# A delta-rule scan on one core: the predictions as 16 products of 128 rows from a block-diagonal state, and solved matrices written row index innermost

## What is computed

```python
rk = x.reshape(Bb, Tt, H, dd)                    # of the layer-normed x
rk = rk / jnp.maximum(jnp.linalg.norm(rk, axis=-1, keepdims=True), 1e-12)
wk = jnp.pad(rk[:, :-1], ((0, 0), (1, 0), (0, 0), (0, 0)))
v = (x @ Wv.T).reshape(Bb, Tt, H, dd)
gate = jax.nn.sigmoid(x @ Wg.T)
beta = jax.nn.sigmoid(x @ Wb.T)
def step(S, inp):
    rk_t, wk_t, v_t, g_t, b_t = inp
    pred = jnp.einsum('bhk,bhkd->bhd', wk_t, S)
    err = (v_t - pred) * b_t[..., None]
    S = S + wk_t[..., None] * err[..., None, :]
    o = jnp.einsum('bhk,bhkd->bhd', rk_t, S) * g_t[..., None]
    return (S, o)
```

## Time and profile before

| | |
|---|---|
| median of 3 runs | 2370.92 us (2365.35 to 2374.8) |
| profiled execution, time | 2373.69 us |
| profiled execution, span | 2372.0 us |
| mean granted TensorE clock | 0.966 of full |
| PE busy | 2108.6 us, 61992 products |
| DVE busy | 1985.7 us |
| ACT, POOL busy | 1727.6 us, 1726.7 us |
| DMA engines, main queue | 30.0% of their time |
| issue of one `kbd` transfer to its landing | 2.0 us (median) |

### The profile page before, as it was taken

The page is one execution under the profiler, slowest core; times in us unless marked ns, Lnnn a source line. Parts: engine busy times, 40 slices in busy tenths (PEclk is TensorE's granted clock), DMA queues, the critical chain, the costliest instruction groups (busy, mean ns, idle before and its releaser), DMA issues. The chain is left out here.

```text
span 2372.0 us, 145909 instructions
## 1 busy us (share of the span) xinstructions
PE 2108.6 (89%) x61992; PEld 1334.4 (56%) x61992; DVE 1985.7 (84%) x5810; ACT 1727.6 (73%) x3628; POOL 1726.7 (73%) x3098
## 2 busy tenths in 40 slices
PE   1679999999999999999999999999999988499997
PEld 1355666566666665656666656666666655255554
DVE  5487899888898888988898888989988985488886
ACT  3767777777777777777777777877777743477775
POOL 2667888888888888888888888888888853144343
PEclk7789999999999999999999999999999997799999
DMA  2111222222222222222222222222222211478885
GB/s 86 51 43 58 76 79 77 75 75 76 78 77 75 74 76 75 76 75 76 76 78 77 75 75 77 78 75 77 77 80 77 59 61 49 151 196 231 227 229 131
DMA packets 132139, 215.53 MB, mean 91 GB/s; under 512 B 31353, under 2 KB 31361, under 8 KB 131489
## 3 DMA queue, kind: packets, MB, share of 16 engines
q1 hardware_dynamic: 131488, 206.20, 30.0%
HBM read 104.40 MB, written 67.11 MB: 72 GB/s over the span
## 5 line engine op out<-in xcount | busy, mean ns | idle before, releaser
L775 DVE TENSOR_TENSOR ps_elim<-ps_elim,sys 128x30 f32<-128x30 f32 (+14 forms) x1920 | 543.6, 326 | 0.8
L783 DVE TENSOR_TENSOR sys<-sys,ps_elim 128x30 f32<-128x30 f32 (+14 forms) x1920 | 534.8, 316 | 1.0
L900 PE MATMUL ps_v<-wv,xt 128*128 128x512 f16 x1536 | 429.7, 390 | 26.1 <-DMA kbd<-kt 13.5
L900 PE MATMUL ps_y<-wo,ot 128*128 128x512 f16 x1536 | 406.9, 388 | 11.6 <-DVE x L827 9.5
L927 PEld LDWEIGHTS ps_chain<-rhs,t_t 32*32 32x32 f32 x16384 | 263.4, 144 | 132.9 <-issue 131.6
L927 PE MATMUL ps_chain<-rhs,t_t 32*32 32x32 f32 x16384 | 296.1, 218 | 24.3 <-issue 18.4
L684 ACT ACTIVATE state<-ps_s 128x512 f32<-128x512 f32 x128 | 76.5, 598 | 265.0 <-PE ps_s L991 265.0
L921 PEld LDWEIGHTS ps_chain<-state,key_t 32*32 32x32 f32 x16384 | 174.8, 105 | 152.6 <-issue 151.1
L991 PEld LDWEIGHTS ps_s<-err,key_b 32*32 32x32 f32 x16384 | 172.6, 107 | 142.9 <-issue 142.3
L1277 PE MATMUL ps_f<-wq,f_xq 128*128 128x512 f16 x1024 | 242.6, 381 | 6.7 <-DVE f_xq L1243 6.7
L803 DVE TENSOR_TENSOR rhs<-val,ps_chain 128x512 f32<-128x512 f32 x128 | 88.0, 687 | 188.3 <-PE ps_chain L921 187.7
(11 more groups left out here) (159 smaller groups left out, 5072.2 us busy)
## 6 DMA issues: line engine op xcount, KB each, us to landing
x_in<-in_L_attn_x SPq DMA_DIRECT2D x128, 256.0 KB
kbd<-kt SPq DMA_DIRECT2D x512, 64.0 KB, 2.0
x_res<-in_L_attn_x SPq DMA_DIRECT2D x128, 256.0 KB
x_scratch<-x SPq DMA_DIRECT2D x128, 256.0 KB, 6.4
f_x<-x_scratch SPq DMA_DIRECT2D x32, 1024.0 KB, 7.7
out<-f_res SPq DMA_DIRECT2D x128, 256.0 KB, 3.8
gate<-gates SPq DMA_DIRECT2D x128, 7.9 KB
gate<-gates SPq DMA_DIRECT2D x128, 0.2 KB
```

Of the source, the lines that this page charges most:

```text
L775: dve.tensor_tensor(tmp, factors(r, c, first, end)[:, c - first:C - 1 - first, c - first:c - first + 1].to_broadcast(shape), sys[:, r, c:c ...
L783: dve.tensor_tensor(dst, dst, tmp, ALU.add).then_inc(elim_done[r], 1)
L900: last = pe.matmul(out, lhs[:, a, kb, :], weights[:, w, kb, :], start=(i == 0), stop=(i == 3 * KB - 1))
```

## The change

Four things change in `attention`.

First, the prediction. `key_t` and its transpose on DVE are gone. `predict` is now 16 products: for each group of 4 heads and each batch, `kt` (128 partitions, 32 columns) is stationary, and the moving side is `state_bd`, the state with its 32x32 blocks on a diagonal of 128 rows and 128 columns. `state_bd` is zeroed once by POOL; after every tile 16 transfers on SP, one for each batch and each head of a group, copy blocks of 32 partitions x 128 numbers from `state` into it. `update` writes its blocks in another order of columns, so that each transfer moves one run of 128 numbers. `kt` has 8 buffers instead of 2, `state` one instead of 2.

Second, the order. On PE, `predict` stands in one piece behind six value products, its waits ahead of the sixth; the second half of `update` comes after one output product instead of three, and the moved ones follow later. On SP, the gate move that waited for its forerunner is issued a step later, the load and the store of rows stand ahead of the `kbd` transfers, and the state's transfers come last in the step, behind `kbd`.

Third, the solved matrices. `t_t` is laid out with the row index innermost, so the 32 numbers that PE loads are neighbours, and DVE's transpose writes them 32 apart.

Fourth, small things: `x_res` has 4 buffers instead of 2, a dump buffer is shared, some semaphores are merged, and `feed_forward` zeroes `y_var` once.

The core of the diff:

```diff
-        t_t = sb("t_t", [P, 2, C, 2, H])
+        t_t = sb("t_t", [P, 2, 2, H, C])
-        state = sb("state", [P, 2, D])
+        state = sb("state", [P, D])
+        state_bd = sb("state_bd", [P, B, HB, KB * HD])
...
+                n, l, live = on(base, j, 0)
+                if live and n < NT - 1:
+                    wait(sp, s["state_done"], n + 1)
+                    for b in range(B):
+                        for i in range(HB):
+                            w = KB * HD * i
+                            sp.dma_start(state_bd[HD * i:HD * i + HD, b, i, :],
+                                         state[C * b:C * b + C, w:w + KB * HD]).then_inc(state_loaded[b][l % 2], 16)
...
-                    nc.scalar.activation(state[:, (l + 1) % 2, :], ps_s[:, :], ACT.Copy).then_inc(s["state_done"], 1)
+                    nc.scalar.activation(state[:, :], ps_s[:, :], ACT.Copy).then_inc(s["state_done"], 1)
...
-                    dve.transpose(t_t[:, r, :, :, :].rearrange("p i a h -> p i (a h)"), sys[:, r, :, :]).then_inc(s["tt_done"], 1)
+                    dve.transpose(t_t[:, r, :, :, :].rearrange("p a h i -> p i (a h)"), sys[:, r, :, :]).then_inc(s["tt_done"], 1)
...
-                    dve.transpose(key_t[:, l, :, :], heads(key[:, l % 2, :])).then_inc(s["keyt_done"], 1)
...
-                    wait(pe, s["state_done"], n + 1)
-                    wait(pe, s["keyt_done"], n + 1)
+                    wait(pe, s["kt_done"], n + 1)
...
+                        for b in range(B):
+                            pe.wait_ge(state_loaded[b][(n - 1) % 2], 64 * ((n - 1) // 2 + 1))
...
-                        for h, q, e in blocks(half):
-                            last = pe.matmul(ps_chain[q, e], key_t[q, l, h, :], state[q, l % 2, e], start=True, stop=True)
+                        for g in range(KB):
+                            for b in range(B):
+                                q, w = slice(C * b, C * b + C), slice(P * g, P * g + P)
+                                moving = state_bd[:, b, :, HD * g:HD * g + HD]
+                                last = pe.matmul(ps_chain[q, w], kt[:, l, g, q], moving, start=True, stop=True)
...
-                            last = pe.matmul(ps_chain[q, e], t_t[q, l // 2 % 2, :, l % 2, h], rhs[q, e], start=True, stop=True)
+                            last = pe.matmul(ps_chain[q, e], t_t[q, l // 2 % 2, l % 2, h, :], rhs[q, e], start=True, stop=True)
...
+                            col = HD * (h % HB * KB + h // HB)
+                            last = pe.matmul(ps_s[q, col:col + HD], key_b[q, l, e], err[q, l % 2, e],
```

More of the change, by code:

```diff
@@ L427, in step @@
                     sp.dma_start(tile(x_in, l % 4), rows(io["x"], base, j, LAG_LOAD)).then_inc(x_loaded[l % 4], 16)
+                n, l, live = on(base, j, LAG_GRAM - 1)
+                if live:
+                    wait(sp, s["gate_moved"], n * 16 + 16)
+                    if isinstance(n, int) and n == 0:
+                        sp.wait_ge(s["zeros"], 3)
+                    sp.dma_start(gate[0:P:C, l, :], gates[C - 1:P:C, (l - 1) % 8, H:2 * H]).then_inc(gate_done[l], 16)
                 n, l, live = on(base, j, LAG_GRAM)
@@ L431, in step @@
                     sp.dma_start(gate[1:P, l, :], gates[0:P - 1, l, H:2 * H]).then_inc(s["gate_moved"], 16)
[L432 to L442, removed]
-                                     kt[HD * i:HD * i + HD, l % 2, :, :]).then_inc(kbd_loaded[l % 2], 16)
                 n, l, live = on(base, j, LAG_Y)
                 if live:
-                    wait(sp, s["x1_done"], n - 1)
-                    sp.dma_start(tile(x_res, l % 2), rows(io["x"], base, j, LAG_Y)).then_inc(res_loaded[l % 2], 16)
+                    wait(sp, s["x1_done"], n - 3)
+                    sp.dma_start(tile(x_res, l % 4), rows(io["x"], base, j, LAG_Y)).then_inc(res_loaded[l % 4], 16)
                 n, l, live = on(base, j, LAG_STATS2)
@@ L452, in step @@
                                  x1[:, l % 4, :]).then_inc(x1_stored[l % 4], 16)
+                n, l, live = on(base, j, LAG_V)
+                if live:
+                    if isinstance(n, int) and n == 0:
+                        sp.wait_ge(s["zeros"], 3)
+                    wait(sp, s["kt_done"], n + 1)
+                    for i in range(HB):
+                        sp.dma_start(kbd[HD * i:HD * i + HD, l % 2, i, :, :],
+                                     kt[HD * i:HD * i + HD, l, :, :]).then_inc(kbd_loaded[l % 2], 16)
+                n, l, live = on(base, j, 0)
+                if live and n < NT - 1:
+                    wait(sp, s["state_done"], n + 1)
+                    for b in range(B):
+                        for i in range(HB):
+                            w = KB * HD * i
+                            sp.dma_start(state_bd[HD * i:HD * i + HD, b, i, :],
+                                         state[C * b:C * b + C, w:w + KB * HD]).then_inc(state_loaded[b][l % 2], 16)
             run(step)
@@ L458, in _ @@
         def _(pool):
-            pool.memset(state[:, 0, :], 0.0).then_inc(s["state_done"], 1)
-            pool.memset(kbd[:, :, :, :, :], 0.0).then_inc(s["kbd_zero"], 1)
-            pool.memset(gates[:, BODY - 1, :], 0.0).then_inc(s["first_gate"], 1)
+            pool.memset(state_bd[:, :, :, :], 0.0).then_inc(s["zeros"], 1)
+            pool.memset(kbd[:, :, :, :, :], 0.0).then_inc(s["zeros"], 1)
+            pool.memset(gates[:, BODY - 1, :], 0.0).then_inc(s["zeros"], 1)
             def step(base, j):
@@ L935, in step @@
                     wait(pe, s["xt_done"], upto(v + 2))
-                value(0, SHARE)
-                last = predict(1)
+                value(0, 2 * SHARE - 1)
+                chain_ready(base, j)
+                value(2 * SHARE - 1, 2 * SHARE)
+                last = predict()
                 if live:
                     last.then_inc(s["pred_psum"], 1)
-                value(SHARE, 2 * SHARE - 1)
                 gram_ready(base, j)
-                value(2 * SHARE - 1, 2 * SHARE)
                 if m_live:
@@ L947, in step @@
                             out = ps_gram[q, :].rearrange("p (i h) -> p h i", h=H)[:, HB * g:HB * g + HB, :]
-                            last = pe.matmul(out, kt[:, m_l % 2, g, q], kbd[:, m_l % 2, :, g, q], start=True, stop=True)
+                            last = pe.matmul(out, kt[:, m_l, g, q], kbd[:, m_l % 2, :, g, q], start=True, stop=True)
                     last.then_inc(s["gram_psum"], 1)
```

74 lines of the change are left out of this document (34 added, 40 removed).

## The result

| | before | changed |
|---|---|---|
| median | 2369.65 us (4 runs) | 3562.83 us (4 runs, 3560.83 to 3564.15) |
| ratio, 95% interval | | 1.5033 [1.5001, 1.5065] |
| profiled execution | 2373.69 us | 3564.15 us |
| mean granted clock | 0.966 | 0.802 |

The change makes the kernel 50% slower. The forecast was 3895 us within 3350 to 4300: the direction and the mechanism were as predicted, the time forecast was 9% too long.

What follows compares the result with a forecast made beforehand. PE's work in written order was taken to bound the kernel at 14.78 us a step; the new transfer link would make the loop 26.7 us. 507.3 + 127 x 26.7, less 2.8, gave 3895 us, range 3350 to 4300.

Steps and rivals of the forecast that it cites:

- held up behind `kbd`: On SP, the state's first transfer waits for the four `kbd` issues ahead of it: 0.6 to 1.5 us, taken as 0.7.
- The link: From state's copy to prediction: 16 transfers issued in series on SP, then landing; takes 15 us and nothing hides it.
- the spacing: On SP, time from one state transfer's issue to the next: 0.62 to 0.92 us, taken as 0.77, 11.55 for 15.
- The clock: PE's clock falls in its pauses, so its 8.6 us in the loop cost 2.4 us more (bounds 0 and 8.6).
- the drain: Drain of the pipeline in the profiled kernel: 65 us with PE busy 49.06 and granted clock 0.77 of full.
- Gaps: PE's issue gaps in the loop: taken as 0.8 us a step, bounds 0 and 1.
- PE's saving: PE's step loses 0.4 us (prediction), 0.7 (solve's layout) and a tenth for issue gaps: 1.2 us, leaving 13.6.
- PE's work in its order sets the pace: Kernel before, steady stretch: PE's work in written order bounds the 14.78 us step, and the scan's loop just fits.
- Hidden transfers: Rival 1: transfers are hidden and PE stays the bound, 2219 us, needing 0.08 us an issue; chance 4%.
- rival (3): Clock stays at 2.4 GHz or SP issues at the faster spacing: 22.4 to 25 us, 3350 to 3680 us; chance 20%.
- the forecast's own: Case (4), the forecast itself: 25 to 28.5 us a step, 3680 to 4125 us; chance 60%.
- all of PE's work in the loop at 1.2 GHz: Rival (6): PE's loop work runs wholly at the low clock, 32.9 us a step, 4680 us; chance 4%.

Runs made afterwards that it cites:

- half_count: Changed kernel with only 8 of the 16 state transfers in each step, that part of the computation left out: 2899.52 us, ratio 1.2181.
- half_bytes: Changed kernel with all 16 state transfers, each of 64 numbers a row instead of 128: 3559.96 us, ratio 1.4956.
- split_queues: Changed kernel with the state transfers of batches 0 and 1 issued by SP, of batches 2 and 3 by ACT: 3091.53 us, ratio 1.2988.
- no_link: Changed kernel without the 16 state transfers; prediction waits only for the state's copy on ACT, state_bd stays zero: 2268.65 us, ratio 0.9614.
- repeat_more: Changed kernel with PE's pause filled: first five value products done eight times more and overwritten (40 added products): 3473.27 us, ratio 1.4718.
- order_and_layout: Kernel before with the change's order on PE and t_t layout, without block-diagonal state and its transfers: 2434.33 us, ratio 1.0262.
- order_only: Kernel before with only the change's order on PE, prediction still of 64 + 64 small products: 2429.07 us, ratio 1.0242.

## Why the prediction was right, point by point

These are the means over the 81 steps between 600 and 2600 us of the changed kernel, each piece taken from its start to the start of the next, in the order of the prediction's sum:

| piece of the loop | predicted us | measured mean us |
|---|---|---|
| held up behind `kbd` | 0.7 | 0.60 |
| first to last issue | 11.55 | 9.80 |
| landing | 2.0 | 1.92 |
| value product and prediction | 1.3 | 2.22 |
| key products, two value products | 1.55 | 2.26 |
| value products and solve | 2.45 | 2.48 |
| transposes, two output products | 1.4 | 1.73 |
| rest of update | 1.9 | 2.57 |
| copy of the state | 0.65 | 0.68 |
| issue gaps, clock | 0.8 + 2.4 | in the rows above |
| sum | 26.7 | 24.27 |

**The link** was the right mechanism: 16 issues in series, each near the price of the earlier trace rows whatever its size, and nothing to hide them. `half_count`, `half_bytes` and `split_queues` each confirm one side of it, and `no_link` shows that it is the whole loss.

**The step that was mis-sized** is the spacing: 0.77 us was the middle of two bursts of four, with a stall in one of them, and the measured mean is 9.80 / 15 = 0.65, near the faster end. For bursts of four 0.77 was right: over the 108 of `kbd` between 300 and 1900 us of the kernel before, the mean is 0.76. The reason given, that a longer burst has no reason to issue better than a short one, was wrong: one `kbd` issue in 6 takes over 0.9 us, but of the state's only one in 41, and a burst of 8 (`half_count`) has as many such stalls as one of 16, 0.4 in mean. Why is open. The spacing is 1.75 of the 2.4 us that the step was too long, 222 us of the 332.

**The clock** fell as forecast, and cost less: 0.92 us on the piece with the prediction and 0.71 on that with the key products, 1.6 against 2.4, since by the solve it was back at the high level. This is another 0.8 us. `repeat_more` puts the clock's cost in these two pieces at 1.8 us. The mean of 0.77 that I took from the drain was that of a stretch with other pauses; the granted clock of the whole run was 0.802, but between 300 and 3000 us 603 us of the time at 1.2 GHz lie in PE's idle, where they cost nothing, and 487 in its work.

**Gaps.** 0.33 us ahead of the output products, mostly PE waiting for DVE's row (`ps_y`, 0.24), and 0.67 in the update, of which 0.38 are pauses for "issue": 1.0 against 0.8.

**PE's saving.** 16 products for 64 and the new layout: 13.99 us a step without the link against 13.6 forecast. But the ledger behind this number was wrong in three places that nearly cancel, and that is luck: the layout alone gives nothing (forecast 0.7 us), the order costs 0.45 us (forecast nothing), and between `order_and_layout` and `no_link` (ratios 1.0262 and 0.9614 of 2370) it is 154 us, 1.2 us a step, where 0.4 were forecast for the prediction's products. The claim that PE's work in its order sets the pace was true only as to PE, not as to its array: part of what was read as a small issue gap is PE waiting for instructions, and it grows when the products get shorter.

**The rivals.** Hidden transfers (2219 us) needed 0.08 us an issue; it was 0.65. The measured 24.1 us a step and 3563 us lie in the band of rival (3), faster spacing or a high clock, 22.4 to 25 us and 3350 to 3680 us, which had a chance of 20%, and not in the forecast's own 3680 to 4125 us, which had 60%. Of (3) the spacing took place; the clock did fall. The case of all of PE's work in the loop at 1.2 GHz did not take place.

## What to carry to other kernels

Price a transfer inside a dependent loop by its issues, counted one by one on the queue that carries them, before its bytes: 16 KB or 8 KB made no difference, 16 or 8 transfers made 5.2 us a step. When PE's idle is put down to "issue" between many small products, compare the products at which the pauses end with the packets of the instruction queue: here PE waited for its instructions, and making each product faster gave nothing, while making them fewer did. A wait long enough to let the clock fall is paid twice, and a run with the pause filled shows how much the second payment is.

## What was not expected of the hardware

In the changed kernel the load of x for the residual, one transfer on SP, takes a median of 3100 ns to issue, where in the kernel before the same form took 602. It is outside of the loop. The state's burst ahead of it is not the whole cause: with a burst of 8 the median is 3040 ns, and in `no_link`, without any burst, it is still 1680. In `order_only`, which keeps the old order on SP, it is 602. The cause is open. The rows of the changed kernel and of `no_link`:

```profile
L442 SPq DMA_DIRECT2D x_res<-in_L_attn_x x128: 532/3100/4186, 202.5 to 3208.9; - x128
...
L442 SPq DMA_DIRECT2D x_res<-in_L_attn_x x128: 532/1680/3407, 167.4 to 1909.9; - x128
```

A block transpose on DVE that writes 32-bit numbers 32 apart took 1907 ns for 128x1024, against 1189 for neighbours. And ACT and DVE copied between different groups of 32 partitions for 0.29 and 0.32 us a block of 32x128 (2.30 and 2.54 us for eight).
